# Last softmax of a graph kernel: the source logits of the last 48 tiles fetched row by row from memory, those of the first 148 still picked with one-hot products

## The reference, cut to what matters

```python
ex = e @ w_edge.T                                   # e: 25,000 x 2
z2 = concatenate([h[src], h[dst], ex], axis=1)
a = leaky_relu(z2 @ w_attn.T, negative_slope=0.01)[:, 0]
a_max = segment_max(a, dst)
a_exp = exp(a - a_max[dst])
denom = segment_sum(a_exp, dst)
attn = a_exp / maximum(denom[dst], 1e-16)
out = segment_sum(attn[:, None] * (ex @ w_e2n), dst)
```

## Time and profile before

| | us |
|---|---|
| median of 3 runs | 3623.36 (3618.66 to 3629.73) |
| the profiled execution's own time | 3626.32 |
| its span in the trace | 3624.6 |
| DVE busy over the span | 2662.3 (73%) |
| PE busy | 2550.8 (70%) |
| POOL busy | 2050.9 (57%) |
| mean granted TensorE clock | 0.855 of full speed |

### The profile page before, as it was taken

The page is one execution under the profiler, slowest core; times in us unless marked ns, Lnnn a source line. Parts: engine busy times, 40 slices in busy tenths (PEclk is TensorE's granted clock), DMA queues, the critical chain, the costliest instruction groups (busy, mean ns, idle before and its releaser), DMA issues. The chain is left out here.

```text
span 3624.6 us, 58127 instructions
## 1 busy us (share of the span) xinstructions
PE 2550.8 (70%) x14623; PEld 1918.8 (53%) x14623; DVE 2662.3 (73%) x8516; ACT 2014.8 (56%) x5963; POOL 2050.9 (57%) x1978
## 2 busy tenths in 40 slices
PE   5567771999577767788588788777768757877530
PEld 2223331666355555577466566655557757776430
DVE  8989982444589799999366677789967759978542
ACT  0023331777322788889466677678867747875110
POOL 7747773776000333343677577577557767720776
PEclk8989995999799898899798899887889979988555
DMA  3435555777199444432566577677678969944321
GB/s 93 102 111 156 153 157 142 244 243 237 48 324 302 144 141 150 142 95 81 154 206 213 173 252 234 223 229 246 195 232 272 260 221 284 294 132 114 88 86 44
DMA packets 521876, 654.00 MB, mean 180 GB/s; under 512 B 99208, under 2 KB 292294, under 8 KB 521544
## 3 DMA queue, kind: packets, MB, share of 16 engines
q1 hardware_dynamic: 455688, 549.38, 48.6%
q0 software_dynamic: 65856, 100.90, 10.3%
HBM read 436.87 MB, written 241.92 MB: 187 GB/s over the span
## 5 line engine op out<-in xcount | busy, mean ns | idle before, releaser
L1620 POOL DMA_INDIRECT look<-table_d,ids x196 | 195.3, 996 | 604.4 <-DVEq L1596 565.4
L1945 POOL DMA_INDIRECT xg_c<-r_d,src_row x392 | 413.0, 1054 | 169.8 <-issue 116.4
L2703 POOL DMA_INDIRECT out<-x_f,out_row x196 | 202.5, 1033 | 174.9 <-DVE x_f L2769 116.0
L1945 POOL DMA_INDIRECT xg_c<-x1d_d,src_row x196 | 216.5, 1105 | 104.9 <-issue 59.4
L1945 POOL DMA_INDIRECT xg_c<-x2d_d,src_row x196 | 202.7, 1034 | 113.4 <-issue 59.1
L925 POOL DMA_INDIRECT xd<-in_x,ids x196 | 216.9, 1106 | 73.1 <-issue 50.3
L1945 POOL DMA_INDIRECT xg_c<-g1d_d,src_row x196 | 201.5, 1028 | 79.0 <-issue 59.1
L550 POOL DMA_INDIRECT rows_d<-row,slot_i x196 | 194.5, 992 | 67.2 <-issue 55.9
L2059 ACT ACTIVATE term_c<-xg_c,scale 128x128 f32<-128x128 f32 x392 | 125.1, 392 | 175.1 <-DMA xg_c<-x1d_d,src_row 102.6
L1964 DVE TENSOR_TENSOR_SCAN agg_t_c<-flags_c,agg_t_c,term_t_c 128x512 f32<-128x512 bf16 x96 | 122.9, 1280 | 102.1 <-ACT term_t_c L2043 64.7
L1964 DVE TENSOR_TENSOR_SCAN agg_t_c<-flags_c,agg_t_c,t_ps_c 128x512 f32<-128x512 bf16 x144 | 183.3, 1273 | 1.8 <-PE t_ps_c L2366 1.8
(11 more groups left out here) (481 smaller groups left out, 9046.6 us busy)
## 6 DMA issues: line engine op xcount, KB each, us to landing
flags_c<-cont_d SPq DMA_DIRECT2D x245, 128.0 KB
xm<-rows_d SPq DMA_DIRECT2D x49, 512.0 KB
m_d<-m_c SPq DMA_DIRECT2D x98, 256.0 KB
r_d<-r_c SPq DMA_DIRECT2D x98, 256.0 KB
m_in_c<-m_d SPq DMA_DIRECT2D x98, 256.0 KB
e_c<-rows_d SPq DMA_DIRECT2D x98, 256.0 KB
x_f<-in_x SPq DMA_DIRECT2D x67, 256.0 KB, 5.5
out<-x_f SPq DMA_DIRECT2D x67, 256.0 KB
```

The source lines that it names most:

```text
L1620: pool.indirect_dma_start(out=look[:, t, :], out_offset=None, in_=table_d[:, :], in_offset=bass.IndirectOffsetOnAxis(ap=ids[:, 0, t:t + 1] ...
L1945: pool.indirect_dma_start(out=xg[:, s, k, :], out_offset=None, in_=table, in_offset=bass.IndirectOffsetOnAxis(ap=src_row[:, t:t + 1], axis=0),
L2703: pool.indirect_dma_start(out=out[:, :], out_offset=bass.IndirectOffsetOnAxis(ap=out_row[:, t:t + 1], axis=0), in_=x4[:, n % SF, k, :], in ...
```

## The change

The 196 tiles are split. The first 37 groups (148 tiles, `PICKED` = 37) are picked as before. For the last 48 tiles, `attn_in` block 1 is lined up once more by PE, copied out of PSUM by DVE into `last_l`, and written by SP to a new table `last_d` of one number for each slot. POOL then issues 48 indirect DMAs, each of which fetches the 128 numbers of one tile by their slot number (`src_line` = 128 `src_tile` + lane) into a column of `under`. SP's write stands behind its first six loads of `lane_b`. `src_line` is made by one DVE instruction in the block at L1664. DVE waits for all 48 fetches before the sum `logit`.

```diff
+        last_d = dram("last_d", [SLOTS, 1])
...
+        src_line = sb("src_line", [P, TILES], I32)
...
                     dve.tensor_copy(lane_l[:, :], p_ps[0:ROWS, 0:LONG]).then_inc(turned_out.sem, 1)
+                    settled(dve)
+                    dve.scalar_tensor_tensor(src_line[:, :], src_tile[:, :], float(P), lane_of[:, :], ALU.mult, ALU.add).then_inc(steps_v.one(), 1)
...
+            PICKED = 37
+            last_l = sb("last_l", [ROWS, LONG], F32, st)
...
                 @block.sync
                 def _(sp):
-                    for n in range(GROUPS):
+                    for n in range(PICKED):
+                        if n == SZ:
+                            sp.wait_ge(last_ready.sem, last_ready.at(2))
+                            sp.dma_start(last_d[:, :].rearrange("(r l) c -> r (l c)", l=LONG), last_l[:, :]).then_inc(last_out.sem, 16)
                         if n >= SZ:
                             sp.wait_ge(apart_made.sem, apart_made.at(n - SZ + 1))
                         sp.dma_start(lane_b[:, n % SZ, :], under_d[0, n * G:(n + 1) * G].partition_broadcast(P)).then_inc(lane_in[n % SZ].sem, 16)
...
                     pool.iota(tile_no_i[:, :], pattern=[[1, TILES]], base=0, channel_multiplier=0).then_inc(steps_g.one(), 1)
+                    pool.memset(under[:, PICKED * K:TILES], 0.0).then_inc(steps_g.one(), 1)
                     pool.wait_ge(steps_g.sem, steps_g.so_far())
+                    pool.wait_ge(last_out.sem, last_out.at(1))
+                    for t in range(PICKED * K, TILES):
+                        pool.indirect_dma_start(
+                            out=under[:, t:t + 1], out_offset=None, in_=last_d[:, :],
+                            in_offset=bass.IndirectOffsetOnAxis(ap=src_line[:, t:t + 1], axis=0),
+                            bounds_check=SLOTS - 1, oob_is_err=False).then_inc(fetched.sem, 16)
...
+                    line_up(pe, l_ps[1][:, 0:LONG], attn_in[:, 1, :]).then_inc(last_ready.sem, 1)
                     line_up(pe, l_ps[0][:, 0:LONG], attn_in[:, 2, :]).then_inc(lined.sem, 1)
                     carry_pe(pe, o_ps[0], seen, 1, 0, 1, 0)
-                    for t in range(TILES):
+                    for t in range(PICKED * K):
...
                     dve.wait_ge(steps_g.sem, tiles_made)
+                    dve.wait_ge(last_ready.sem, last_ready.at(1))
+                    dve.tensor_copy(last_l[:, :], l_ps[1][0:ROWS, 0:LONG]).then_inc(last_ready.sem, 1)
                     dve.tensor_copy(tile_no[:, :], tile_no_i[:, :]).then_inc(steps_v.one(), 1)
...
-                    for t in range(TILES):
+                    for t in range(PICKED * K):
                         dve.wait_ge(picks.sem, picks.at(t + 1))
...
-                    dve.wait_ge(pick_read.sem, pick_read.at(TILES))
+                    dve.wait_ge(pick_read.sem, pick_read.at(PICKED * K))
+                    dve.wait_ge(fetched.sem, fetched.at(TILES - PICKED * K))
                     settled(dve)
                     dve.tensor_tensor(logit[:, :], part[:, :], under[:, :], ALU.add).then_inc(logits_up.sem, 1)
```

More of the change, by code:

```diff
@@ L2547, in graph_kernel @@
             logits_up = signal("logits_up")
+            PICKED = 37
+            last_l = sb("last_l", [ROWS, LONG], F32, st)
+            last_ready, last_out = signal("last_ready"), signal("last_out", 16)
+            fetched = signal("fetched", 16, "pool_queue")
             lane_in = [signal(f"lane_in{s}", 16) for s in range(SZ)]
@@ L2593, in _ @@
                     act.wait_ge(minus_ready.sem, minus_ready.at(1))
-                    for it in range(GROUPS + 1):
+                    for it in range(PICKED + 1):
                         n = it
-                        if n < GROUPS:
+                        if n < PICKED:
                             act.wait_ge(lane_in[n % SZ].sem, lane_in[n % SZ].at(n // SZ + 1))
@@ L2601, in _ @@
                         n = it - 1
-                        if 0 <= n < GROUPS:
+                        if 0 <= n < PICKED:
                             if n >= 3:
```

## The result

| | before | after |
|---|---|---|
| median of 15 runs each, us | 3621.52 (3616.96 to 3629.73) | 3631.87 (3618.38 to 3641.60) |
| the profiled execution | 3626.32 | 3631.41 |
| its span | 3624.6 | 3629.4 |

The ratio of the runs is 1.0025, with a 95% interval of 1.0013 to 1.0037: some 9 us slower, where 3 us less were forecast. The median lies above the range of 3611 to 3629.

A forecast was written before the change was run, and what follows sets the result against it. The softmax block, paced by DVE's picks, was taken to pass its gain to the end in full; POOL's fetches would bound it after. `logit` -4.0 and transposes +0.75 gave -3.3 us: median 3620.1, range 3611 to 3629.

The forecast's parts named there:

- the price of `src_line`: Block ahead of the next block's first load: one DVE instruction of some 0.4 us, fitting into 2.1 us of cover.
- The first paragraph: What bounds the kernel: the softmax block's saving or loss reaches the end in full; DVE's picks set its pace.
- the sum: Whole kernel: `logit` 4.0 us earlier, transposes 0.75 us slower, together -3.3 us, with bounds of -6.7 and +0.1.
- Picks: DVE in the softmax block: 148 picks at 0.345 us each, starting about 0.9 us later and ending at 3298.1.
- Start of POOL: Softmax block: first fetch at 3246.35 (between 3242.9 and 3248.3), after the write of `last_d` behind six loads.
- The lower end: Earliest release by the write of `last_d`, if it overtook the loads: 3242.0, with the first fetch at 3242.9.
- Spacing: POOL's 48 fetches in the softmax block: 1.30 us from one to the next, last one ending at 3308.45.
- Landing: After the last fetch ends: 1.46 us until its numbers are there, at 3309.9; the skill's fit about 0.5 us later.
- The logit: End of the softmax block's picks and fetches: starts at 3309.9 instead of 3313.92, after DVE waits about 12 us.
- Cold transposes: PE's six transposes behind `logit`: at clock 0.50 after the idle gap, 0.23 us apart and 0.42 long, costing 0.75 us.
- Rival 1: Softmax block: DVE's picks hold up POOL's fetches, +8.2 us at half a pick each, +16.6 at a whole; chance 0.10.
- Rival 2: Softmax block: fetches keep up with picks at 1.05 us spacing, `logit` at 3298.1, -15.8 us, 3607.5 in all; chance 0.05.

The follow-up runs named there:

- base_again: The kernel before, run again unchanged beside the kernel before: 3624.33 us against 3624.16, ratio 1.0001 (0.9990 to 1.0012).

## Why the prediction was wrong

**The step that failed** is the price of `src_line`. The list of what the change adds costs it as "one DVE instruction of some 0.4 us", and not as a tile of 800 bytes that moves every tile behind it. The first paragraph, "what the softmax block saves or loses, the end gains or loses in full", hid this: it held for what stands behind that block (the block began 8.1 us late and the last one 5.2 us late, and the span is 4.8 us longer), but the sum took all that stands ahead of it as it was. The instruction itself was priced right: it took 0.35 us, and the next block's first load came 2.14 us after the write of `under_d` was issued, where it was 2.13. The term of the place of the tiles was put at nothing, and it measured +12.1 us in the second attention block of the profiled execution, +6 to +13 over all the shifted kernels. With it and the softmax block as measured, the sum for the profile is 3626.3 - 2.9 + 12.1 = 3635.5, and 3631.4 was measured; some 4 us were won elsewhere ahead of the softmax block, as much as `base_again` differs from before. The 15 runs agree: 9 us slower by the ratio, with a softmax block that is 2.9 us shorter, leaves 12 us for the rest. The last sentence of the prediction, that such a time "would say that another stage moved", is what happened, but neither the range nor a rival had it.

**The local terms**, in the order of the prediction, with 8.13 us taken off the times after:

- Picks: 3254.89 to 3306.72 for 147 steps, less 1.1 us of waits for PE, is 0.345 us each, as forecast. They end at 3299.0, forecast 3298.1.
- Start of POOL: 3246.13, forecast 3246.35. The write went out at 3239.91 as said. The sixth load landed at 3244.98, and POOL began 1.15 us after that. The lower end, by which the write would overtake the loads, is excluded here. That the start fits within 0.2 us has some luck in it: the loads were through 1.2 us later than forecast, and by the wake of 0.85 us the write needed 0.3 us more and not the 1.7, for which no row stood.
- Spacing: 1.30 us, 48 fetches of 1.00 us on average. Right, though "All of POOL's indirect DMAs cost about the same" passes over the slower ones in the profile of before: the gathers of L1945 take 1.03 to 1.11 us on average, and those of L925 1.11.
- Landing: the last fetch ends at 3316.58 and the logit starts at 3318.55, 1.97 us and not 1.46. The Trainium skill (DMA: Bandwidth & Descriptors, Anatomy of one DMA) fits about 2.0 us of fixed cost, and the trace agrees with it; the one gather behind which ACT waited was too good a case.
- The logit: 3310.42 against 3313.92, -3.5 us, forecast -4.0. DVE waited 11.4 us, forecast 12. The profile puts that down to "issue", where "a DMA" was forecast.
- Cold transposes: 0.21 to 0.25 us apart and 0.42 to 0.46 long, as forecast. The block gained 2.9 us, forecast 3.3.

**Rival 1** (POOL held up by the picks) was wrong everywhere: 1.00 us on average and 0.30 us between on every chip, beside 148 picks with hardly a gap on the 3624 us chips. The longest single fetch took 1.22 us. What it had right is only that picks and fetches can disturb each other, and that came the other way round, on the 4300 us chips, at 40 us. **Rival 2** needed 1.05 us from one fetch to the next; the shortest distance was 1.30.

## What to carry to other kernels

A new persistent tile is not free even when its instruction is. Look at the addresses of the tiles behind it, above all those of stages whose DMA share is near 1, as here (0.98). Here it was enough to keep them on multiples of 512 bytes of a partition, by padding or by using dead space. When an edit's own block shows what was forecast and the total doesn't, compare the starts of the same instructions over the whole trace first; that finds the stage. A balance of work between POOL's fetches and the other engines that is tuned on one chip should be measured on another one before it is trusted.

## What was not expected of the hardware

- The second attention block, which DMA bounds, runs at 304 to 309 GB/s with its tiles at multiples of 512 bytes and at 286 to 296 with them 32 or 64 bytes past a multiple of 256; a packet of 2048 bytes takes 98 to 103 and 107 to 111 ns.
- On the chips of three of the five batches the same program took 19 to 20% longer (4315 to 4354 against 3624 us). Most of it arose where POOL issues indirect DMAs, from 15 us in 511 (the lookups) to 76 in 260 (a stage of gathers).
- Beside a row of indirect DMAs of POOL DVE waited up to 5.2 us for a product there, while POOL itself ran at its usual pace.
